# Experts that gather rows by a token table made with one-hot products, and two passes of the graph stage moved to ScalarE

## What is computed

```python
# graph: similarity of the context's tokens, cut at each row's 153rd largest
sim = einsum('bhnd,bhmd->bnm', Q, K) / (sqrt(d) * H)
A = sigmoid(sim) * (sim >= top_k(sim, 153)[0][:, :, -1:])
x = x + (1 - gamma) * layernorm(x) + gamma * (A + A.T) * 0.5     # gamma = sigmoid(gamma_raw)

# experts: 32 routed (and 32 that pass nothing), 8 choices a token, 256 rows an expert
scores = softmax(layernorm(x) @ w_cls.T);  topk_idx = top_k(scores + bias, 8)[1]
w = normalised scores of the choices * 1.5
buf[e, pos] = layernorm(x)[token]       # pos: how many choices before this one went to e; dropped from 256 on
y = (silu(g) * u) @ w_down[e],  g, u = split(buf[e] @ w_gate_up[e])
out[token] = sum_k w_r[k] * y[expert_k, pos_k] * (1 + weights of the choices that pass nothing)
```

## Time and profile before

| | |
|---|---|
| median of three runs | 3042.47 us (3036.84 to 3046.91) |
| profiled execution, its own time | 3039.41 us |
| its span, first to last instruction | 3037.4 us |
| mean granted TensorE clock | 0.899 |
| graph stage | 668.8 to about 1159 us |
| experts stage | about 1162 to 1482 us |
| busy in the span | PE 81%, DVE 60%, ACT 41%, POOL 28% |

### The profile page before, as it was taken

The page is one execution under the profiler, slowest core; times in us unless marked ns, Lnnn a source line. Parts: engine busy times, 40 slices in busy tenths (PEclk is TensorE's granted clock), DMA queues, the critical chain, the costliest instruction groups (busy, mean ns, idle before and its releaser), DMA issues. The chain is left out here.

```text
span 3037.4 us, 34907 instructions
## 1 busy us (share of the span) xinstructions
PE 2468.5 (81%) x12662; PEld 1636.9 (54%) x12662; DVE 1837.5 (60%) x2917; ACT 1242.0 (41%) x1873; POOL 855.3 (28%) x1198
## 2 busy tenths in 40 slices
PE   5898989863443356999448999999999869999999
PEld 4454545321221135999334554545555538888887
DVE  3766576627888964777557777565655544444443
ACT  2444444328656624666203433344333323333332
POOL 2232222215578773333443332001211110000000
PEclk8999999976665677999768999999999979999999
DMA  3213131227122245999585656333433323101000
GB/s 117 64 43 84 43 84 46 70 77 287 62 97 92 84 161 180 305 304 303 173 182 138 157 147 156 88 89 100 113 95 92 102 85 133 42 1 42 1 28 14
DMA packets 200952, 340.40 MB, mean 112 GB/s; under 512 B 28809, under 2 KB 60425, under 8 KB 198754
## 3 DMA queue, kind: packets, MB, share of 16 engines
q1 hardware_dynamic: 177250, 299.80, 32.5%
q0 software_dynamic: 20480, 37.87, 5.1%
q10 hardware_dynamic: 3072, 0.79, 0.1%
HBM read 182.30 MB, written 109.05 MB: 96 GB/s over the span
## 5 line engine op out<-in xcount | busy, mean ns | idle before, releaser
L757 DVE TENSOR_REDUCE at_negmax<-at_ps 128x2 f32<-128x1024 f32 (+3 forms) x256 | 259.1, 1016 | 120.7 <-PE at_ps L523 63.7
L670 ACT ACTIVATE at_probs<-at_ps 128x1024 f32<-128x1024 f32 (+3 forms) x256 | 221.7, 866 | 269.9 <-PE at_ps L538 267.6
L1367 DVE TENSOR_REDUCE a_negmax<-a_ps 128x2 f32<-128x1024 f32 x128 | 155.1, 1217 | 137.0 <-PE a_ps L1120 136.4
L1896 ACT ACTIVATE gr_act_signs<-gr_signed,gr_test 128x512 bf16<-128x512 f32 x248 | 177.2, 716 | 81.5 <-POOL gr_test L2236 53.4
L59 PE MATMUL ff_ps<-ff_xnT_hi,ff_s_hi 128*128 128x512 f32 x512 | 201.1, 393 | 5.1 <-DVE ff_xnT_lo L2766 5.1
L61 PE MATMUL ff_ps<-ff_xnT_hi,ff_s_lo 128*128 128x512 f32 x512 | 200.4, 391 | 0.0
L60 PE MATMUL ff_ps<-ff_xnT_lo,ff_s_hi 128*128 128x512 f32 x512 | 200.4, 391 | 0.0
L538 PE MATMUL at_ps<-at_qk 98*128 98x512 f32 (+3 forms) x512 | 172.1, 418 | 21.2 <-DMA at_qk<-at_mrow 11.5
L2796 DVE TENSOR_TENSOR ff_hid<-ff_hid,ff_ps 128x512 f32<-128x512 f32 x64 | 44.0, 688 | 238.6 <-ACT ff_hid L2741 238.6
L1268 ACT ACTIVATE a_probs<-a_ps 128x1024 f32<-128x1024 f32 x128 | 130.9, 1023 | 135.1 <-PE a_ps L1138 134.6
L518 PE MATMUL at_ps<-at_qk 96*128 96x512 f32 (+3 forms) x512 | 162.4, 381 | 19.5 <-DVE at_xnT_lo L818 8.9
(11 more groups left out here) (410 smaller groups left out, 6557.1 us busy)
## 6 DMA issues: line engine op xcount, KB each, us to landing
at_qk<-at_part SPq DMA_DIRECT2D x384, 128.0 KB, 2.5
first_gu<-in_L_ffn_w_gate_up_dram SPq DMA_DIRECT2D x32, 1024.0 KB, 5.6
a_qk<-a_part SPq DMA_DIRECT2D x192, 128.0 KB, 2.3
slot_rows<-gr_zeros SPq DMA_DIRECT2D x16, 1024.0 KB
first_d<-in_L_ffn_w_down_dram SPq DMA_DIRECT2D x32, 512.0 KB, 6.5
ex_rows<-slot_rows SPq DMA_DIRECT2D x32, 512.0 KB, 4.6
out_rows<-ex_y SPq DMA_DIRECT2D x32, 512.0 KB, 3.1
gr_aside_raw<-in_L_ffn_W_dram SPq DMA_DIRECT2D x48, 256.0 KB, 3.1
```

The source lines that it names most:

```text
L670: act.activation(probs[:, t % 2, 2 * w:2 * w + 2, lo:S], banks(("kq", g, s), lo), ACT.Exp, scale=SCALE).then_inc(free(("kq", g, s)), 1)
L757: dve.reduce_max(negmax[:, g % 2, :].rearrange("p (j t) -> p j t", t=NT)[:, 2 * w:2 * w + 2, t], banks(("qk", g, s), 0, width(g, t)), AX.X ...
L1367: dve.reduce_max(negmax[:, g % 2, :].rearrange("p (j t) -> p j t", t=NT)[:, 2 * w:2 * w + 2, t], banks(("qk", g, s)), AX.X, negate=True).t ...
L1896: act.activation(act_signs[:, j, :], src, ACT.Sign, scale=-1.0, bias=against, accum_out=total[:, i, j:j + 1]).then_inc(counted_to[j], 1)
```

## The change

Scatters and zeroing go. The normalised rows are stored whole to a DRAM tensor `normed` (row 0 zero, one row a token), and each expert's rows are gathered from it by an `index` of tokens, by GpSimd in the experts stage. The index is made so: VectorE splits each token's position in each expert (`place`) into a block of 32 and a row in it (`block_of`, `row`); GpSimd turns both into one-hot tensors in bf16; TensorE multiplies them (`table`), which sums token numbers into slots; VectorE adds the batches (`add_table`), and TensorE moves the result to its partitions (`move_tokens`). For the last batch VectorE makes the rows' one-hot tensor itself (`last_rows`). Beside that the blend of x and the normalising go from VectorE to ScalarE (`blends`, `normals`), at rounds 2 and 8 of the next batch; `keep_normed`, `keep_logits` and `exponentials` move from rounds 9, 11, 13 to 11, 13, 15; the second power goes to round 7. `hot` becomes bf16, `prod` has half its size.

```diff
 # SyncE, graph stage
-            many = slot_rows.rearrange("(p q r) d -> q p (r d)", p=P, r=zeros.shape[1] // D)
-            for q in range(ZERO_DMAS):
-                sp.dma_start(many[q], zeros[:]).then_inc(zeroed, 16)
+            def store_normed(b):
+                sp.wait_ge(xn_done, NT * (b + 1))
+                sp.dma_start(normed_tiles[b], xn[:, b % 2]).then_inc(normed_out, 16)
 # TensorE
+            def table(b):
+                pe.wait_ge(logT_copied, b + 1)
+                pe.wait_ge(blocks_set, b + 1)
+                if b < B - 1:
+                    pe.wait_ge(rows_set, ROW * (b + 1))
+                else:
+                    pe.wait_ge(vector_rows, 1)
+                for t in range(NT):
+                    for g in range(GROUPS):
+                        e = SIDE * g
+                        mm = pe.matmul(ps[:, LOGT, g * P // 2:(g + 1) * P // 2], rows_hot[:, t, e:e + SIDE, :].rearrange("p e r -> p (e r)"),
+                                       block_hot[:, :, t, e:e + SIDE, :], start=t + g == 0, stop=t == NT - 1 and g == GROUPS - 1, skip_group_check=True)
+                mm.then_inc(tabled, 1)
+            def move_tokens():
+                pe.wait_ge(index_step, 1)
+                by_side = token_of[:].rearrange("p g (t w) -> p w g t", w=SIDE)
+                for h in range(SIDE):
+                    for w in range(SIDE):
+                        mm = pe.matmul(ps[ROW * w:ROW * (w + 1), MOVED, h * GROUPS * HALVES:(h + 1) * GROUPS * HALVES], env.ident[:, ROW * h:ROW * (h + 1)],
+                                       by_side[:, w], start=True, stop=True, skip_group_check=True)
+                mm.then_inc(moved, 1)
             for b in range(B):
                 transposed_adjacency(b)
+                if b:
+                    pe.wait_ge(tab_added, SIDE * b)
...
                 run_asides(b + 1)
+                if b + 1 < B:
+                    table(b)
             for u, (j, c) in enumerate(late_units):
+                if u == len(LATE_BANKS):
+                    table(B - 1)
+                    move_tokens()
 # ScalarE
+            def blends(b):
+                act.wait_ge(blending[0], 3 * (b + 1))
+                if b:
+                    act.wait_ge(stored, 16 * b)
+                for t in range(NT):
+                    act.activation(xo[:, t, :], xs[:, t, :], ACT.Identity, scale=blend[:, 2, t:t + 1], bias=blend[:, 1, t:t + 1]).then_inc(blended[0], 1)
+            def normals(b):
+                act.wait_ge(blending[1], b + 1)
...
+                for t in range(NT):
+                    act.activation(xn[:, b % 2, t, :], xo[:, t, :], ACT.Identity, scale=rstd[:, 1, t, 0:1], bias=blend[:, 3, t:t + 1]).then_inc(xn_done, 1)
+                    if b and r == 2:
+                        blends(b - 1)
+                    if b and r == 8:
+                        normals(b - 1)
             sigmoids(B - 1)
+            blends(B - 1)
             for n in asides(B - 1)[ROUND_ASIDES:]:
                 keep_aside(n)
+            normals(B - 1)
             keep_normed(B - 1)
 # VectorE
-                for t in range(NT):
-                    dve.tensor_scalar(xo[:, t, :], xs[:, t, :], blend[:, 2, t:t + 1], blend[:, 1, t:t + 1], ALU.mult, ALU.add).then_inc(blended[0], 1)
-                for t in range(NT):
-                    dve.tensor_scalar(xn[:, b % 2, t, :], xo[:, t, :], mv[:, 1, t, 0:1], rstd[:, 1, t, 0:1],
-                                      ALU.subtract, ALU.mult).then_inc(xn_done, 1)
+                dve.scalar_tensor_tensor(out=blend[:, 3, :], in0=mv[:, 1, :, 0], scalar=-1.0, in1=rstd[:, 1, :, 0], op0=ALU.mult, op1=ALU.mult
+                                         ).then_inc(blending[1], 1)
+            def add_table(b):
+                dve.wait_ge(tabled, b + 1)
+                for h in range(SIDE):
+                    here = slice(ROW * h, ROW * (h + 1))
+                    new = ps[here, LOGT, :].rearrange("p (g n h k) -> p h g n k", n=2, h=SIDE, k=BLOCKS)[:, h]
+                    if b:
+                        dve.tensor_tensor(found[here], found[here], new, ALU.add).then_inc(tab_added, 1)
+                    else:
+                        dve.tensor_copy(found[here], new).then_inc(tab_added, 1)
                 blend_x(b)
+                if b:
+                    add_table(b - 1)
                 strike_out(b + 1, 0, 2)
+                    # in places(), after the position sums
+                    dve.tensor_scalar(row[:], flat, 1.0 / ROW, 0.5 / ROW - 0.5, ALU.mult, ALU.add).then_inc(decoding, 1)
+                    dve.tensor_scalar(block_of[:], row[:], 1.5 * 2.0 ** 23, 1.5 * 2.0 ** 23, ALU.add, ALU.subtract).then_inc(decoding, 1)
+                    dve.scalar_tensor_tensor(out=row[:], in0=block_of[:], scalar=-float(ROW), in1=flat, op0=ALU.mult, op1=ALU.add).then_inc(decoding, 1)
+                    dve.scalar_tensor_tensor(out=row[:], in0=row[:], scalar=1.0, in1=chosen, op0=ALU.add, op1=ALU.mult).then_inc(decoding, 1)
+            def last_rows():
+                dve.tensor_tensor(rows_hot[:].rearrange("p t e r -> p (t e) r"), bcast_mid(row_iota[:], NT * E_ROUTED),
+                                  bcast_last(row[:], NT * E_ROUTED, ROW), ALU.is_equal).then_inc(vector_rows, 1)
 # GpSimd, graph stage: all scatters go, and
+            def row_hot(b, n):
+                pool.tensor_scalar(rows_hot[:].rearrange("p t e r -> p (t e) r")[:, :, n], row[:], n + 1.0, None, ALU.is_equal).then_inc(rows_set, 1)
+            def blocks_hot(b):
+                for n in range(BLOCKS):
+                    pool.tensor_scalar(in_block.rearrange("p (e k) -> p e k", k=BLOCKS)[:, :, n], block_of[:], float(n), None, ALU.is_equal).then_inc(numbers, 1)
+                pool.tensor_tensor(block_hot[:, 1].rearrange("p t e k -> p t (e k)"), in_block.rearrange("p (t m) -> p t m", t=NT),
+                                   bcast_last(tile_no[:, NT * b:NT * (b + 1)], NT, E_ROUTED * BLOCKS), ALU.mult).then_inc(numbers, 1)
+                pool.tensor_scalar(in_block, in_block, token[:, 0:1], None, ALU.mult).then_inc(blocks_set, 1)
+                    if b and r >= WRITE_AT:                       # WRITE_AT, A_ROUND = 23, 3
+                        for v in range(A_ROUND * (r - WRITE_AT), A_ROUND * (r - WRITE_AT + 1)):
+                            row_hot(b - 1, v)
+                if b:
+                    for v in range(A_ROUND * (TESTS - WRITE_AT), ROW):
+                        row_hot(b - 1, v)
+                    blocks_hot(b - 1)
                 rstds(b, 0)
 # experts
-                sp.dma_start(rows[:, u], rows_dram[bass.ds(e, 1)].rearrange("e p t d -> (e p) t d")).then_inc(rows_in[u].sem, 16)
+            def gather(e):
+                i, u = e // 2, e % 2
+                turned[u].wait(pool, i, 0)
+                for t in range(CT):
+                    at = CT * (E_ROUTED // SIDE * (e % SIDE) + e // SIDE) + t
+                    pool.indirect_dma_start(rows[:, u, t, :], None, normed, bass.IndirectOffsetOnAxis(index[:, at:at + 1], 0)).then_inc(rows_in[u].sem, 16)
+            gather(0)
+            gather(1)
             split_d(0, 0)
             split_d(0, 1)
+            gather(2)
             for e in range(E_ROUTED):
+                if e + 3 < E_ROUTED:
+                    gather(e + 3)
```

More of the change, by code:

```diff
@@ L1736, in _ @@
             sp.wait_ge(stored, 16 * B)
[L1737 removed]
+            store_normed(B - 1)
             late_load(sp, 3)
@@ L2400, in turn @@
             def turn(i, u, after):
-                rows_in[u].wait(pe, i, 16)
+                rows_in[u].wait(pe, i, 16 * CT)
                 if after is not None:
```

162 lines of the change are left out of this document (98 added, 64 removed).

## The result

The changed kernel takes 3163.2 us (median of 4 runs, 3155.7 to 3164.5) where the kernel before takes 3041.3: a ratio of 1.0395, 95% interval 1.037 to 1.0419. It is 122 us slower. I had forecast 3022 and a range up to 3048. The profiled execution took 3164.5 us, its span is 3162.7.

What follows compares the result with a forecast made beforehand. VectorE was taken to bound the graph stage's loop over batches and GpSimd's scatters its end. Terms -1.5 - 13.1 + 14.9 + 11.3 - 31.5 - 0.6 = -20.5 gave 3019 us profiled, 3022 for runs, range 3008 to 3048.

Steps and rivals of the forecast that it cites:

- Experts: Experts stage: 64 gathers on GpSimd replace SyncE's loads, are issued two experts ahead and cost 0.
- rival (c): Experts: with DMA engines 89% busy, TensorE waits 0.5 us for each expert, 16 us in all, 3038; chance 0.07.
- GpSimd's one-hots: Threshold search and after it: each row or block operation of 128 takes 0.34 us, giving rounds of 2.5 us.
- rival (b): GpSimd's one-hots cost 1.1 us each by the row of 23, 0.9 taken; rounds 4.2 us, total 3075; chance 0.11.
- the loop: Graph stage, loop over batches: less waiting and work for VectorE, so batch 3 starts its finish 13.1 us earlier.
- Batch 3 up to its router: Last batch: ScalarE's blends delay the asides, then table and transposed adjacency; with the normalising, +14.9 us.
- Router to the last copy: Last batch's end: VectorE's decoding and comparison of 4096, GpSimd's blocks, then table sums and moves in series; +11.3 us.
- the scatters' tail: Last copy to the experts' queue: 34.6 us of scatters, landing, drain and signals shrink to 3.1; -31.5 us.
- first rows: Start of the experts: the first gather starts before the queue's signals end; -0.6 us.
- Start: Before the graph work: the 16 zeroing DMAs of 1 MB go, and with them a ScalarE wait; -1.5 us.
- Rival (a): Loop: VectorE's masking and adjacency hold GpSimd's last blocks, power 3.5 us late in three batches; 3037; no chance stated outright.

Runs made afterwards that it cites:

- gather_ahead: The changed kernel with GpSimd issuing the gathers of expert e+4, not e+3, before it splits the weights of e+2; 3088.9 us, ratio 1.0159 to the kernel before.
- packed_hots: gather_ahead with GpSimd's one-hot operations writing results side by side, not at a stride (token table then wrong); 3055.3 us, ratio 0.9995 to the kernel before.
- one_hots_on_vector: The changed kernel with VectorE making both one-hots of every batch, only the two block products left on GpSimd; 3112.4 us, ratio 1.0247 to the kernel before.
- ahead_swap: gather_ahead with ScalarE keeping the last batch's six asides before the blends instead of after; ratio 1.0114 to the kernel before.
- power_first: gather_ahead with GpSimd's power for the blend before the last five row operations and the blocks, instead of after; ratio 1.0114 to the kernel before.
- gpsimd_forms: gather_ahead with ten extra GpSimd operations of different forms at the start of the graph stage, while VectorE is idle; run once, 3097.4 us.

## Why the prediction was wrong

The forecast said -20.5 us, the spans of the profiled executions say +125.3: 5.8 before the stage, 43.1 in it, 76.3 in the experts, 0.1 behind.

- **Experts, 0 forecast, +76.3.** The step that failed is "issued two experts ahead, and cost 0 there". I counted GpSimd's idle time and looked at the DMA share, as in rival (c), and took the distance from the loop's index. In the queue each gather stands behind the split for the expert two before it, which waits for ScalarE, which waits for TensorE's down product. Counted along the queue: the split ends 15.3 us after the transposing before last (1377.04 to 1392.34), the gathers are issued behind it, the rows are there 8.4 us after the first issue, 3.3 us too late, every second expert. The waits are 51.5 us in 15, and some 1.6 us at the lower clock behind each make 24 more: together 75.5. gather_ahead showed it by changing the order alone. Rival (c) had the place and the sign right, with the wrong cause (load of the DMA engines) and a price of 0.5 us an expert where it was 2.4.
- **GpSimd's one-hots, 0.34 us forecast, 1.03 measured.** The second step that failed, and my rival (b) by its size: its row of 23 gave 7 ns an element, and the strided form costs 6.1. That the two agree is luck. The row of 23 is written side by side, in which form 128 results take 0.53 us and not the 1.1 that I drew from it; what costs 6.1 is the stride, of which rival (b) says nothing. I had set it aside because "no other one-input row is dearer than 0.92 ns"; but that other row was a select, which writes side by side, and I compared neither the stride nor the kind of operation. Rounds came to 4.78 us (rival (b) 4.2, forecast 2.5), the wait for the coefficients to 15.7 in each of batches 1 to 3 (rival (b) 16). For the loop that is +36.0 instead of -14.6; rival (b)'s total was +53 on the forecast, where 43.1 + 20.5 = 63.6 came. packed_hots and one_hots_on_vector bring batch 3 back to 400.4 and 396.0.
- **Batch 3 up to its router, +14.9 forecast, +26.0 measured.** The mechanism (blends, then asides, then table, then transposed adjacency) was right, and ahead_swap shows it. The term missed the late power, which begins the chain: the coefficients came 23.0 us into the finish (1107.80 to 1130.83) and not 7.2, 15.8 later. The chain from the last blend to the transposing was 7.6 us instead of 10.2, and from there to the router 1.1 us went where I had added 1.3, so 11 of the 15.8 us were left. Without the late power (one_hots_on_vector) the way was +10.4.
- **Router to the last copy, +11.3 forecast, +11.8 measured; the scatters' tail -31.5 and first rows -0.6, together -32.1 forecast, -30.7 measured.** Right, though the terms listed for the first of them add up to 10.8 and not 11.3. The comparison of 4096 took 4.42 us (4.4 forecast).
- **Start, -1.5 forecast, -1.3 measured.** Right.
- **Rival (a)**, that VectorE holds GpSimd, is true in its mechanism and small in the loop: with the operations side by side the coefficients are 7.0 us late (it said 3.5), some 1.4 of it by holding. The holding shows best in the tail. In one_hots_on_vector GpSimd's product of 1024, which takes 1.89 us in the loop, took 6.01 beside VectorE's comparison of 4096 with its two inputs:

```profile
1122.99 4.42 DVE L2267 TENSOR_TENSOR gr_rows_hot<-gr_row_iota,gr_row 128x4096 bf16<-128x4096 f32 x1
...
1123.16 6.01 POOL L2355 TENSOR_TENSOR gr_block_hot<-gr_block_hot,gr_tile_no 128x1024 bf16<-128x1024 bf16 x1 [24.80 <-DVE gr_block_hot L2265]
```

6.01 - 1.89 = 4.1 us of holding for a pass of 4.42. The Trainium skill, "SBUF — State Buffer", section "Who interferes with whom", says that a two-input VectorE operation and a GpSimd operation that reads SBUF exclude each other for the whole instruction; this row agrees.

With the gathers one expert earlier and the one-hots side by side (packed_hots), the same structure comes to a ratio of 0.9995 and not to the forecast's 0.993. By the marks its first rows are 22 us behind the forecast (498.3 against 476.2), of which VectorE's three waits for the coefficients are 21, and its experts take 11.8 us more than before: the late start that gather_ahead has too, and the gaps whose cause is open. That is more than the ratio's 20 us; the marks of the kernel before are from an earlier execution.

## What to carry to other kernels

Work that moves to an idle engine stands in that engine's queue: write down what is in front of it there, what that waits for, and when the result is then ready against its reader, before calling it "two ahead". A price from a neighbouring row holds only if the operation, the number of inputs, the size and the stride of the output are the same. Here the select's row was too low (0.34 us against 0.53 side by side) and the row of the same operation, at 23 elements, too high for that form (1.1) and right for the strided one by chance; where the nearest rows lie between 0.9 and 7 ns an element and forty operations a batch depend on it, the form itself has to be timed first. And before a long wait is blamed on what it names, look what stands ahead of that in its queue: power_first changed the name of 16 us and none of its length.

## What the runs showed of the hardware

- A GpSimd comparison with one f32 input and 128 results takes 0.53 us when they lie side by side and 1.0 us at a stride of 8 or 32 (in the kernel, by the 96, 0.54 and 1.03); a two-input product of the same size takes 0.40 and a copy 0.30 (gpsimd_forms, one row each).
- The rows of an indirect gather of 128 rows issued by GpSimd land 6.8 us after the issue (changed kernel, median of 64, with the weights' loads beside them), SyncE's plain load of twice as many rows after 4.6 (kernel before, median of 32).
- A wait of 3.3 us costs TensorE 4.9 (changed kernel, at 1400.86): in the 3.6 us after it the products run at 0.41 us instead of 0.28, with a granted clock of 0.54. Over a stretch of 48 us with two such waits the clock is 0.93, and 1.00 in gather_ahead, which has none.
- A GpSimd product of two inputs (1024 elements, bf16) takes 6.01 us instead of 1.89 when it starts beside a VectorE comparison of 4.42 us that has two inputs (one_hots_on_vector).
